# Attention scores of a 1-core Trainium2 kernel: from two terms over 128 rows to three terms over 64 rows, two score tiles at a time

## The reference, cut to what matters

```
x:   (8, 224, 512)    ctx: (8, 750, 512)    Wq, Wk, Wv, Wo: (512, 512)
q = (layernorm(x) @ Wq).reshape(B, N, 8, 64)
k = (ctx @ Wk).reshape(B, M, 8, 64);  v = (ctx @ Wv).reshape(B, M, 8, 64)
sim  = einsum('bihd,bjhd->bhij', q, k) * 64 ** -0.5
attn = softmax(sim, axis=-1)
x    = x + tanh(g_xattn) * (einsum('bhij,bjhd->bihd', attn, v).reshape(B, N, 512) @ Wo + bo)
# then: experts. h = gelu(x_ln @ w1[e] + b1[e]); y = h @ w2[e] + b2[e]; all 8 experts summed, one gate per token
x    = x + tanh(g_ffn) * (sum over e of y_e) * norm_gate(x_ln)
```

## Time and profile before

| | |
|---|---|
| median of three runs | 1821.06 us (1819.58 to 1828.24) |
| span of the profiled execution | 1816.1 us, from its first to its last instruction |
| PE matmul busy | 1794.9 us, 99% |
| PE weight load busy | 1615.8 us, 89% |
| DVE busy | 1330.5 us, 73% |
| ACT busy | 810.9 us, 45% |
| POOL busy | 1184.1 us, 65% |
| TensorE clock granted | 1.000 of full speed (2.4 GHz) |

### The profile page before, as it was taken

How to read it: one execution, slowest core, us unless ns; L and a number is a source line. 1 busy time by engine, 2 the same in 40 slices (tenths; PEclk the granted TensorE clock), 3 DMA queues, 4 the chain that set the end, 5 groups by cost and what they waited for, 6 DMA issues and landing times.

```text
span 1816.1 us, 31801 instructions
## 1 busy us (share of the span) xinstructions
PE 1794.9 (99%) x9720; PEld 1615.8 (89%) x9720; DVE 1330.5 (73%) x2308; ACT 810.9 (45%) x1574; POOL 1184.1 (65%) x900
## 2 busy tenths in 40 slices
PE   7999999999999999999999999999999999999999
PEld 7999999999999878888888888888888888888887
DVE  7888878888888877666666766588766767676657
ACT  6767677677766832323232323243232323232322
POOL 5525445263544679777777777699877777777743
PEclk9999999999999999999999999999999999999999
DMA  5111202021120222111111111123412121212111
GB/s 176 39 41 36 57 22 61 21 62 40 34 69 16 92 97 74 66 54 62 58 58 58 58 58 58 47 66 106 127 57 63 52 69 47 69 46 69 46 47 53
DMA packets 52057, 110.35 MB, mean 61 GB/s; under 512 B 13208, under 2 KB 25496, under 8 KB 52000
## 3 DMA queue, kind: packets, MB, share of 16 engines
q1 hardware_dynamic: 52000, 109.64, 19.3%
HBM read 98.61 MB, written 11.01 MB: 60 GB/s over the span
## 4 chain that ended last, share of the span: by engine, by line
PE 96%; DVE 1%; issue 1%; ACT 1%; DMA 0%; SPq 0%; POOL 0%; ACTq 0%; DVEq 0%
PE bank L781 33%; PE scores L754 28%; PE bank L625 19%; PE scores L696 5%; PE bank L706 4%; PE bank L718 4%; PE bank L632 1%; PE scores L839 0%; DVE h_sum L1051 0%; DMA ctx_raw<-in_ctx 0%; ACT hs L1318 0%; PE bank L754 0%; ACT probs L1190 0%; DVE xs L900 0%; ACT h_full L1317 0%
## 5 line engine op out<-in xcount | busy, mean ns | idle before, releaser
L781 PE MATMUL bank<-w2s,hs 128*128 128x512 f32 x2688 | 620.9, 389 | 1.3 <-DVE xres L1018 1.0
L781 PEld LDWEIGHTS bank<-w2s,hs 128*128 128x128 f32 x2688 | 504.4, 188 | 105.1 <-issue 1.5
L754 PE MATMUL scores<-xs,w1s 128*128 128x448 f32 x2646 | 549.5, 366 | 3.6 <-DVE h_sum L1051 3.5
L754 PEld LDWEIGHTS scores<-xs,w1s 128*128 128x128 f32 x2646 | 495.8, 188 | 48.7 <-DVE h_sum L1051 3.8
L1051 DVE TENSOR_TENSOR h_sum<-scores,h_sum 128x448 f32<-128x448 f32 x441 | 262.7, 619 | 183.3 <-PE scores L754 182.8
L1317 ACT ACTIVATE h_full<-h_sum,b1T 128x448 f32<-128x448 f32 x256 | 170.9, 668 | 303.1 <-DVE h_sum L1051 292.4
L1066 DVE TENSOR_TENSOR acc<-bank,acc 128x512 f32<-128x512 f32 x337 | 229.1, 686 | 71.5 <-PE bank L781 62.9
L900 DVE TENSOR_TENSOR hs<-h_full,hs 128x448 fp32r<-128x448 f32 x256 | 237.9, 930 | 52.2 <-ACT hs L1318 52.1
L1190 ACT ACTIVATE h_sum<-scores 128x448 f32<-128x448 f32 x63 | 34.3, 545 | 475.4 <-PE scores L754 475.4
L1391 POOL TENSOR_SCALAR probs<-probs,row_inv 112x750 f32<-112x750 f32 x60 | 130.6, 2176 | 100.1 <-DVE row_inv L989 100.1
L1493 POOL CAST w1s<-w_stage 128x768 fp32r<-128x768 f32 x64 | 69.0, 1078 | 168.5 <-PE scores L754 168.5
(11 more groups left out here) (128 smaller groups left out, 2197.3 us busy)
## 6 DMA issues: line engine op xcount, KB each, us to landing
w_stage<-in_L_ffn_w SPq DMA_DIRECT2D x128, 512.0 KB, 3.5
ctx_raw<-in_ctx SPq DMA_DIRECT2D x16, 376.0 KB, 3.2
ctx_raw<-in_ctx SPq DMA_DIRECT2D x14, 374.0 KB, 3.2
xa<-in_x SPq DMA_DIRECT2D x16, 224.0 KB, 2.7
xres<-in_x SPq DMA_DIRECT2D x16, 224.0 KB, 2.7
x_scratch<-xres SPq DMA_DIRECT2D x16, 224.0 KB, 2.3
xt_scratch<-yT SPq DMA_DIRECT2D x16, 224.0 KB, 2.8
x_raw<-xt_scratch SPq DMA_DIRECT2D x4, 896.0 KB, 7.7
```

The source lines that it names most:

```text
L754: mm = pe.matmul(product_bank(g, name)[:, 0:TH], w1s[j % 2][:, s, W_OF[name], kc, :], xs[:, i, m, kc, :], start=n == 0, stop=n == 5)
L781: mm = pe.matmul(bank[:, :], hs[j % 2][:, s, ht, t * P:(t + 1) * P], w2s[j % 2][:, m, ht, :], start=n == 0, stop=n == 5)
```

## The change

Keys and queries of two neighbouring heads are now stored as a pair: the even head in rows 0 to 63, the odd head in rows 64 to 127, with high and low part one behind the other along the free dimension. That is how the projections leave PE, so ACT and DVE drain each `K` and each `Q` item with one instruction over 128 rows. A score tile is now three terms (high x high, high x low, low x high) over the 64 rows of its head, so six matmuls instead of four. Two tiles are issued together: query tile 1 of head h (one row half) and query tile 0 of head h+1 (the other row half), matmul by matmul in turn; they go to the two score tiles of PSUM. The first tile of the first batch and the last tile of the last batch stand alone. The waits of both tiles stand ahead of the pair. The size of the tiles is unchanged.

```diff
-            qst[0] = a("queries0", [P, 2, G, NQ], F32R)
+            qst[0] = a("queries0", [P, G, 2, NQ], F32R)
...
                 elif kind == "S":
                     _, _, h, qt = item[:4]
-                    g, hh = h // G, h % G
-                    pe.wait_ge(lo_out["K"], number(("K", db, g, hh // 2, 1), b))
-                    pe.wait_ge(lo_out["Q"], number(("Q", db, g, hh // 2), b))
-                    if not (isinstance(b, int) and n <= 2):
-                        pe.wait_ge(exp_out, n - 2)
-                    rows = slice(qt * QT, (qt + 1) * QT)
-                    for k0, k1 in HALVES:
-                        for s in range(2):
-                            last = pe.matmul(ps_scores[qt][0:QT, SCORES.start + k0:SCORES.start + k1],
-                                             qst[g][:, s, hh, rows], kst[g][:, hh, k0:k1], start=s == 0, stop=s == 1)
+                    pair = [(h, qt, db)]
+                    if qt == 1 and not (isinstance(b, int) and b + db == B - 1 and h == H - 1):
+                        pair.append((h + 1, 0, db) if h < H - 1 else (0, 0, db + 1))
+                    for h_, qt_, db_ in pair:
+                        n_ = number(("S", db_, h_, qt_), b)
+                        pe.wait_ge(lo_out["K"], number(("K", db_, h_ // G, h_ % G // 2, 1), b))
+                        pe.wait_ge(lo_out["Q"], number(("Q", db_, h_ // G, h_ % G // 2), b))
+                        if not (isinstance(b, int) and n_ <= 2):
+                            pe.wait_ge(exp_out, n_ - 2)
+                    for half, (k0, k1) in enumerate(HALVES):
+                        for term, (s, m) in enumerate(((0, 0), (0, 1), (1, 0))):
+                            for h_, qt_, db_ in pair:
+                                here = slice(64 * (h_ % 2), 64 * (h_ % 2) + 64)
+                                last = pe.matmul(ps_scores[qt_][0:QT, SCORES.start + k0:SCORES.start + k1],
+                                                 qst[h_ // G][here, h_ % G // 2, s, qt_ * QT:(qt_ + 1) * QT],
+                                                 kst[h_ // G][here, h_ % G // 2, m, k0:k1],
+                                                 start=term == 0, stop=term == 2)
+                                if half == 1 and term == 2 and (h_, qt_, db_) != pair[-1]:
+                                    last.then_inc(in_psum["S"], 1)
...
                 elif kind == "K":
-                    sub(kst[g][64:128, 2 * p, keys], bank[0:64, 0:n], kst[g][0:64, 2 * p, keys])
-                    last = sub(kst[g][0:64, 2 * p + 1, keys], bank[64:128, 0:n], kst[g][64:128, 2 * p + 1, keys])
+                    last = sub(kst[g][:, p, 1, keys], bank[:, 0:keys.stop - keys.start], kst[g][:, p, 0, keys])
```

The `Q` drains change in the same way, and the high halves on ACT too. The written lists are new throughout; one line of the body list of PE stands for them:

```diff
-        K1.0.0 S2.0 S2.1 T0.0 T0.1 T0.2 O<0 K1.1.0 P0 S3.0 T1.0 T1.1 K1.0.1 S3.1 Q1.0 O<1 T1.2 V1.0 Y<0 K1.1.1
+        K1.0.0 T0.0 T0.1 T0.2 O<0 K1.1.0 P0 T1.0 S2.1 K1.0.1 Q1.0 T1.1 O<1 V1.0 Y<0 T1.2 K1.1.1 P1 T2.0 S3.1
```

More of the change, by code:

```diff
@@ L121 @@
+        Y<1 T2.1 V1.1 T2.2 V1.2 V1.3 Q1.1 P2 T3.0 S4.1 T3.1 T3.2 V1.4 P3 V1.5 V>0.0 S5.1 T4.0 T4.1 V>0.1 T4.2
+        V>0.2 X>0 P4 X>1 S6.1 T5.0 T5.1 Q>0.0 K>0.0.0 T5.2 K>0.1.0 K>0.0.1 V>0.3 P5 T6.0 S7.1 V>0.4 T6.1 T6.2
+        Q>0.1 P6 K>0.1.1 T7.0 T7.1 V>0.5 T7.2 S>0.1 P7 S>1.1
     """),
     "act": plan("""
-        K1.0.0 T0.0 M1.0 T0.1 T0.2 S2.0 K1.1.0 P0 S2.1 T1.0 M2.0 T1.1 K1.0.1 Q1.0 S3.0 T1.2 V1.0 S3.1 Y<0 K1.1.1
-        P1 T2.0 Y<1 T2.1 T2.2 S4.0 M3.0 S4.1 V1.1 Q1.1 V1.2 V1.3 M4.0 P2 T3.0 T3.1 T3.2 P3 S5.0 V1.4 M5.0 V1.5
@@ L136 @@
+        V>0.1 R5.1 T4.2 A>0.1 R6.0 V>0.2 X>0 X>1 D4 T5.0 T5.1 S6.1 Q>0.0 K>0.0.0 S7.0 T5.2 R6.1 R7.0 K>0.1.0
+        V>0.3 K>0.0.1 D5 S7.1 T6.0 S>0.0 R7.1 V>0.4 T6.1 T6.2 D6 Q>0.1 T7.0 K>0.1.1 T7.1 V>0.5 T7.2 S>0.1
+        R>0.0 S>1.0 R>0.1 S>1.1
     """),
     "pool": plan("""
-        D<7 M1.1 L<1.0 L<1.1 M2.1 D1 M3.1 C>0.0 C>0.1 L>0.0 L>0.1 M4.1 D3 M5.1 C>1.0 C>1.1 M6.1 D5 M7.1 M>0.1
+        D<7 M1.1 L<1.0 M2.1 L<1.1 M3.1 L>0.0 D1 C>0.0 C>0.1 M4.1 C>1.0 L>0.1 M5.1 D3 C>1.1 M6.1 D5 M7.1 M>0.1
@@ L144 @@
     "pe": plan("""
[L145 to L148, removed]
+        K1.0.0 T0.0 T0.1 T0.2 O<0 O<1 P0 Q1.0 S2.1 Q1.1 T1.0 K1.1.0 Y<0 K1.0.1 T1.1 T1.2 K1.1.1 P1 T2.0 V1.0
+        S3.1 T2.1 T2.2 V1.1 V1.2 P2 T3.0 T3.1 S4.1 T3.2 V1.3 V1.4 P3 V1.5 S5.1 T4.0 T4.1 Y<1 T4.2 P4 S6.1 T5.0
@@ L149 @@
+        T5.1 T5.2 S7.1 B0 P5 T6.0 T6.1 T6.2 H0 H1 H2 P6 T7.0 T7.1 T7.2 H3 P7 H4 H5 H6 O0 O1
     """),
     "act": plan("""
[L151 to L154, removed]
+        K1.0.0 T0.0 T0.1 T0.2 S2.0 M1.0 P0 Q1.0 Q1.1 T1.0 S2.1 Y<0 K1.1.0 K1.0.1 T1.1 M2.0 T1.2 S3.0 P1 T2.0
@@ L162 @@
+        T5.0 S7.0 D4 R6.1 T5.1 T5.2 S7.1 R7.0 B0 D5 R7.1 U2 T6.0 T6.1 U3 T6.2 U4 H1 H2 D6 T7.0 U5 T7.1 T7.2 U6
+        D7 H3 H4 H5 H6 O0 O1 L1.0 L1.1 A1.0 A1.1
     """),
     "pool": plan("""
-        D<7 M1.1 L<1.0 L<1.1 Z F M2.1 D1 M3.1 W0.0 G0 G1 G2 W0.1 W0.2 D3 W0.3 G3 W0.4 D5 W1.0 D7 W1.1 W1.2 W1.3
-        W1.4 L1.0 L1.1
+        D<7 L<1.0 L<1.1 M1.1 F M2.1 M3.1 D1 Z G0 G1 W0.0 G2 W0.1 D3 W0.2 W0.3 W0.4 D5 G3 W1.0 D7 W1.1 W1.2
+        W1.3 W1.4 L1.0 L1.1
     """),
@@ L955, in drain @@
                     keys = slice(*HALVES[half])
-                    n = keys.stop - keys.start
-                    sub(kst[g][64:128, 2 * p, keys], bank[0:64, 0:n], kst[g][0:64, 2 * p, keys])
-                    last = sub(kst[g][0:64, 2 * p + 1, keys], bank[64:128, 0:n], kst[g][64:128, 2 * p + 1, keys])
+                    last = sub(kst[g][:, p, 1, keys], bank[:, 0:keys.stop - keys.start], kst[g][:, p, 0, keys])
                 elif kind == "Q":
                     _, _, g, p = item
-                    for odd in range(2):
-                        src = slice(64 * odd, 64 * odd + 64)
-                        for to in range(2):
-                            last = dve.scalar_tensor_tensor(
-                                qst[g][64 * to:64 * to + 64, 1, 2 * p + odd, :], bank[src, 0:NQ], DH ** -0.5,
-                                qst[g][src, 0, 2 * p + odd, :].bitcast(F32), ALU.mult, ALU.subtract)
+                    last = dve.scalar_tensor_tensor(qst[g][:, p, 1, :], bank[:, 0:NQ], DH ** -0.5,
+                                                    qst[g][:, p, 0, :].bitcast(F32), ALU.mult, ALU.subtract)
                 elif kind == "V":
@@ L1260, in hi @@
                     keys = slice(*HALVES[half])
-                    n = keys.stop - keys.start
-                    copy(kst[g][0:64, 2 * p, keys], bank[0:64, 0:n])
-                    last = copy(kst[g][64:128, 2 * p + 1, keys], bank[64:128, 0:n])
+                    last = copy(kst[g][:, p, 0, keys], bank[:, 0:keys.stop - keys.start])
                 elif kind == "Q":
                     _, _, g, p = item
-                    for odd in range(2):
-                        for to in range(2):
-                            last = copy(qst[g][64 * to:64 * to + 64, 0, 2 * p + odd, :],
-                                        bank[64 * odd:64 * odd + 64, 0:NQ], scale=DH ** -0.5)
+                    last = copy(qst[g][:, p, 0, :], bank[:, 0:NQ], scale=DH ** -0.5)
                 elif kind == "V":
```

47 lines of the change are left out of this document (22 added, 25 removed).

## The result

The changed kernel took 1862.28 us (median of 4 runs, 1859.2 to 1862.92) against 1823.61 us for the kernel before on the same occasions: ratio 1.0218, interval 1.0193 to 1.0244. Forecast were 1826 us and a range from 1799 to 1850; the time lies above both.

What follows compares the result with a forecast made beforehand. PE, busy 99% of the span, was taken to bound the kernel: 1816.1 - 20.9 + 24.0 + 3.2 - 1.5 = 1820.9 us span, with 5.0 us from span to median 1826 us; range 1799 to 1850.

Steps and rivals of the forecast that it cites:

- new waits: Body: a pair waits for both score tiles; their exponentials, 7 us or more of PE work earlier, cost nothing.
- The prediction's own sign: Body: PE waits exceeding 4 us by much would show the forecast wrong, in favour of rival 5.
- Slots and halves at once: Score pairs: row halves run at once, six slots of 0.171 us, 1.03 us a pair, 0.34 less than before.
- rivals 1, 3 and 4: Pairs: 1, half loads in turn, 1837 us, 20%; 3, halves not at once, 1887, 11%; 4, own-half loads unhidden, 1867, 7%.
- The late start of the second half: Inside a pair: second half's first load starts behind the first half's, 0.05 us taken, 3.2 us over 63.
- The change-over: 65 score runs: PE entering and leaving 64-row matmuls costs 0.37 us a run, 24.0 us in all.
- rival 2: Score runs: change-over to 64 rows costs little; 1802 us without it, 1814 with half of it; chance 18%.
- The sign: Ahead of score runs: 65 load-engine idle times of about 0.3 us by issue, a stream and some 0.1 us.
- The three terms together: Score products on PE: 20.9 us less for the products, 24.0 more for change-overs, 3.2 more for late starts.
- Start and end of attention: PE's waits at both ends of attention: 1.5 us gained for both, from 4 gained to 3 lost.
- rival 5: Transposes behind a pair: shorter lead makes them late, 0.4 us for each of 56 heads, 22 us; 1848 us; chance 6%.
- The 2.6 us: From head 7's last score tile to its first transposes: left for queueing, 7.0 us of cover against a 4.4 us chain.

Runs made afterwards that it cites:

- the later pair: Changed kernel with the pair (1.1, 2.0) moved from a batch's end to behind the next batch's first transposes; 1845.02 us, ratio 1.0119.
- the last experiment: The kernel with both pairs moved, with DVE and ACT finishing head 7's transposes ahead of reciprocals and scaling; 1837.52 us, ratio 1.009.
- The kernel with both pairs moved: Changed kernel with S>0.1 six groups ahead of P7, S1.1 behind the next batch's K1.0.0, DVE's C0.1 ahead of the layernorm items; 1843.14 us, ratio 1.0134.

## Why the prediction was wrong

The step that failed is the one on new waits: "Those exponentials belong to the pair before, 7 us or more of PE work earlier, and cost nothing." That holds for seven pairs of a batch, which start 7.7 us or more behind the pair before. At the eighth, `S>0.1 P7 S>1.1`, there are 1.2 us of PE work between. The chain there, from the first pair's end at about 191.6 over the maxima to the second exponential's end at 195.0, is 3.4 us, so about 2 us of wait follow; the terms 0.93 and 0.89 for maximum and exponential stood in the earlier trace rows, and I had set them against the usual distance between two pairs, not against the shortest. Taking the place away took the wait and the low clock away (the later pair, 17 us). Seven such waits, with the clock behind them, are 7 x 3.7 = 26 of the 45 us. The prediction's own sign, waits of PE in the body far above 4 us, came true (12.4 us), but it stood for late transposes, which was another cause.

The second thing missing was a price for what follows a wait. I priced waits at their length. Here 2.07 us of wait brought 3.4 us at the lower level of the clock, 1.6 us more. With 0.2 us for the pairs that makes 3.9 us a batch of the 4.3; the rest lies in shorter delays. In the kernel before there was no such stretch in the body (1.00 in the earlier trace rows).

Point by point:

- *Slots and halves at once.* Right. A pair's steps are 0.171 us, its twelve matmuls take six, its loads go side by side; rivals 1, 3 and 4 fell. The late start of the second half, put at 0.05 us a pair, is 0.003. The first step, 0.26, holds the first load, which stands in the sum under the change-over.
- *The change-over.* Right in the sum. The first matmul behind a change-over is on record while its load still runs, so I read to the second start. From the last transpose to the pair's second step are 0.467 us in the changed kernel, and to the second score matmul 0.285 before; from the last score matmul to the second matmul of the keys behind it 0.531 instead of 0.344. That is 0.18 and 0.19, 0.37 us together; rival 2 fell. The sign was only half right: the load engine's idle time by issue is 0.25 us behind the pair (209.26), but only 0.11 us ahead of it when transposes come before, since a transpose's own turn is short. From the last transpose to the first 64-row load are 0.20 us, its turn of 0.11 and 0.09.
- *The three terms together* were put at -20.9 + 24.0 + 3.2 = 6.3 us. Without the late start, which the trace doesn't show, they are 3.1 us, and the 0.03 us a pair read from the traces (1.40 for 1.37) agree. So the new products explain about 3 of the 45 us.
- *From span to time.* The 5.0 us that I added are not a fixed distance: each run of the kernel before is some 2.0 us longer than its span (1822.38 and 1820.4), the changed kernel's 1.8 (1862.92 and 1861.1); the rest was the spread of the runs.
- *Beside PE.* 70.3 us less on DVE for the 72 forecast, worth nothing in itself, as said.
- *Start and end of attention.* Mis-sized: -1.5 us, from -4 to +3, against +3.6 ahead of the first P0 and +8.8 behind the last. The head's part is C0.1 behind the layernorm items, shown by putting it back. In the end list PE waits 1.20, 1.07 and 1.16 us in a row and the clock falls again; the ten microseconds below alone, at 0.57 and 0.50, cost some 4 us of busy time, more than the three waits last:

```profile
652.71 1.92 PE L726 MATMUL bank<-probsT,values 125*128 125x448 f32 x6 [1.20 <-DVE probsT L908]
658.74 1.12 PE L714 MATMUL bank<-ident,probs 112*125 112x112 f32 x8 [1.07 <-ACT yT L1192]
661.02 2.18 PE L700 MATMUL scores<-keys,queries 64*112 64x376 f32 x6 [1.16 <-ACT probs L1236]
```
```profile
660.00:665.00 5.00, 3.98 (x8) 0.57 0.67 204
665.00:670.00 5.00, 5.00 (x20) 0.50 0.14 58
```

- *The shorter lead to the transposes (rival 5).* Not in the changed kernel, whose body has no such wait. It came with the later pair, 1.28 us once a batch: there the transposes of head 0 follow too soon on their own pair. The 2.6 us had been worked out for head 7 in the changed order.

The last experiment's span, 1835.7 us, splits the whole. It is 19.6 us over before, of which some 3 are the products; the other 16 or so are waits, slow clock and shorter delays, over half of them in the first batch (5.0 us) and behind the last P0 (some 7.5 us). The other 25 of the 45 us were the order of the changed kernel's lists, some 18 us of it in the batches behind the first and the rest at the start and the end. That the products alone would have given 1826 us or less in a kernel without any of these waits is an extrapolation; no run reached it.

## What to carry to other kernels

Where a change makes an instruction wait for two buffers instead of one, check each place in the order list where the distance is shortest, the seams between loop iterations first; the usual distance hides it. Price a wait on a busy TensorE at its length and what the clock does behind it, read from the granted clock, and take the length from the starts of its matmuls: the idle time was 0.28 us where 0.45 were lost. And where one wait ends an engine's slack, moving it makes the next one late: the wait moved three times here (2.07, then 1.28 or 1.20, then 0.29 us), so a new order wants all its engines' lists redone.

## What the runs showed of the hardware

- Two matmuls over 64 rows in different row halves run fully at once, 3 to 4 ns apart, with their loads side by side: 0.171 us for both at 376 columns, the same as one over 128 rows. Across the halves they need not keep program order (six ahead of six: nine steps, 1.40 us).
- Going from matmuls over 112 or 128 rows to 64 and back costs 0.37 us a pair, half on the way in and half on the way out; as often as it was made here, 65 times, its 24 us ate the whole gain of the shorter product, 20.9 us.
- A wait of 2.07 us was followed by 3.4 us at the lower level of the clock, seven times out of seven. With the tiles one after the other a wait of 1.6 us came in each batch, and the low clock only in every second. Single waits of 1.20 and 1.28 us in the body of two experiments were followed by none: both bodies read 1.00. But at the start of attention in the last experiment a wait of 1.27 us, with one of 0.25 ahead of it, was (the first two rows and the windows). The kernel with both pairs moved has the same two waits at the same place (the third row), and its clock reads 1.00 from 40 to 60 us:

```profile
43.10 0.68 PE L726 MATMUL bank<-probsT,values 125*128 125x448 f32 x2 [0.25 <-DVE probsT L908]
45.05 0.66 PE L714 MATMUL bank<-ident,probs 112*125 112x112 f32 x4 [1.27 <-POOL probs L1388]
44.05 0.66 PE L714 MATMUL bank<-ident,probs 112*125 112x112 f32 x4 [1.27 <-POOL probs L1388]
```
```profile
44.00:46.00 2.00, 0.95 (x8) 1.00 0.17 60
46.00:48.00 2.00, 2.00 (x15) 0.59 0.03 8
48.00:50.00 2.00, 2.00 (x8) 0.56 0.00 0
```

So the length of the wait alone doesn't decide whether the clock falls behind it. What does, no run here shows.
